# Adaptive layer norm block on one core: preparation joined with the projections, modulation applied by ScalarE, values stored without ones

## The chip, the cores and the metric

One core of a Trainium2 chip runs the whole program in one launch. The metric is the device time in microseconds (us). TensorE (PE) multiplies matrices, VectorE (DVE) and ScalarE (ACT) work on tiles, GpSimd (POOL) works on tiles in on-chip memory, and SyncE (SP) issues transfers (DMAs). All tensors are float32; some operands of matmuls are marked fp32r.

## The reference, cut to what matters

A batch of 8 sequences of 1024 tokens with 256 channels goes through a 16-head attention and a two-layer windowed block, each behind a modulated layer norm. The change concerns the first part:

```python
x = L0_attn_x                                            # 8 x 1024 x 256
mod = (_silu(L0_c) @ L0_wmod).reshape(8, 6, 1, -1)
sa, ca, ga, sb, cb, gb = (mod[:, 0], ..., mod[:, 5])
ga = (2 * (ga >= 0) - 1) * jnp.maximum(jnp.abs(ga), 0.25)   # gb likewise
h = _layernorm(x, axis=-1) * (1 + ca) + sa
# attention of h:
q = x @ wq.T                      # 16 heads of 16 channels, rotated by an angle that depends on the head
k = x @ wk_a.T @ wk_b.T           # through 64 latent channels, rotated too
v = x @ wv_a.T @ wv_b.T
attn = softmax(q k^T / 4)
x = x + ga * ((attn @ v) @ wo.T)
```

The angle depends on the head, not on the token, so the rotation is folded into the weights.

## The kernel before

The program is a row of blocks. At the end of a block all engines meet, and the block's stores must have landed.

**setup** loads the weights, transposes them on TensorE, rotates `wq` and `wkb` on VectorE, computes the 8 x 1536 modulation and stores it in DRAM (`mod_d`), and prepares a table `trl` for the later windowed block. Every engine waits for all 23 loads (`loaded`, `total`).

**projections** goes over 16 chunks of 512 tokens. For each chunk n, SP loads `pj_x` (512 KB) and `pj_mod` (a broadcast of two rows of `mod_d`). VectorE makes the statistics in 12 dependent steps (L365 to L88) and normalizes into `pj_xn` (L498). GpSimd multiplies by 1 + ca and adds sa in two passes (L534) into `pj_hm`. TensorE transposes it (L554, eight 128x128 turns), ScalarE copies `pj_hT` out (L601), TensorE makes the 128 latent channels (L563), q (L570), k (L577) and v (L585). ScalarE copies the high parts of q and k (L611, L613) and v (L619). VectorE subtracts to get the low parts (L504, once for q and once for k). SP stores four tiles of parts (L468, 512 KB each) and v (L471). Every value head of 16 channels is stored with 16 ones beside it, so that one matmul later gives both the weighted sum and the softmax's denominator; `pj_v` is therefore 1024 KB a chunk. VectorE works two chunks ahead with the normalization, in slices between the two low parts, and TensorE turns one chunk ahead.

**full_attention** goes over 32 groups (batch x 4 heads) of 16 steps. TensorE computes the scores twice, once for the row maxima (L803, reduced by VectorE at L923) and once transposed (L822) for ScalarE's exponential (L896), and then the sums with the values (L837). SP loads q, k and v of group n + 2 while group n runs. GpSimd has only the split of the next stage's weights there (L1205, L1210), once, in group 9.

**attention_out** (16 chunks of 512 tokens) and four later blocks follow; the change leaves their code as it is.

The lines around which the change turns:

```python
def body(n, p, following=True):                       # TensorE, projections
    pe.wait_ge(h_ready.sem, h_ready.upto(n))
    ...                                               # latents L563, q L570
    pe.wait_ge(lat_ready.sem, lat_ready.upto(n))
    ...                                               # k L577
    if following:
        turn(n + 1, 1 - p)
    ...                                               # v L585
```

Of the kernel before, what the change touches and what calls it, by code (L numbers as in the profile page):

```python
# [7 lines left out]
ALU = mybir.AluOpType  # L8
# [7 lines left out]
P = 128  # L16
# [116 lines left out]
def build(nc, a, out):  # L133
    with ExitStack() as ctx:
# [5 lines left out]
        v_d = dram("v_d", [B, N, NH * 2 * HD])  # L140
# [52 lines left out]
def setup(nc, a, ident, w, mod_d, trig_d, hi_d):  # L193

    with ExitStack() as ctx:
        def sb(name, shape, dt=F32):
            return ctx.enter_context(nc.sbuf_tensor(name, shape, dt))

        def sem(name):
            return ctx.enter_context(nc.semaphore(name))  # L200

        wq_r = sb("wq_r", [P, KT, D])
        wo_r = sb("wo_r", [P, KT, D])
        wa_r = sb("wa_r", [P, D])
        wb_r = sb("wb_r", [P, KT, P])
        rope = sb("rope_b", [P, 2, P])
        ropeq = sb("rope_q", [P, 2, P])
        ta, tb = sb("rope_ta", [P, KT, P]), sb("rope_tb", [P, KT, P])
        cs = sb("c_rows", [B, D])
        ce = sb("c_exp", [B, D])  # L210
        cT = sb("c_T", [P, KT, B])
        wmod = sb("wmod_sb", [P, KT, 6 * D])
        mods = sb("mods", [B, 6, D])
        ga, gs = sb("guard_a", [B, 2, D]), sb("guard_s", [B, 2, D])
        trig = sb("trig_base", [P, NW, 4 * DH])
        qks = sb("qk_scales", [P, DEPTH, 4 * DH])
        trl = sb("trig_scaled", [P, DEPTH, NW, 4 * DH])
        zrow = sb("zero_rows", [B, P])
        ps = [ctx.enter_context(nc.psum_tensor(f"ps_set{i}", [P, 512], F32)) for i in range(8)]
        loaded, turned, steps, silu, stored = (sem("set_loaded"), sem("set_turned"), sem("set_steps"),  # L220
                                               sem("set_silu"), sem("set_stored"))
        small, modm = sem("set_small"), sem("set_mod")
        n_loads = [0]

        with nc.Block() as block:
            @block.sync
            def _(sp):
                def load(dst, src):
# [25 lines left out]
                for h in hi_d:  # L254
                    sp.dma_start(h[:, 0, :], zrow[:]).then_inc(stored, 16)
# [1907 lines left out]
```

## Time and profile before

| what | value |
|---|---|
| time, median of 3 runs | 4484.74 us (4481.17 to 4498.85) |
| time of the profiled execution | 4477.03 us |
| its span, first to last instruction | 4475.2 us |
| mean granted TensorE clock, as a share of full | 0.973 |
| busy: PE / DVE / ACT / POOL | 92% / 80% / 62% / 36% |
| HBM read and written | 178.56 MB and 111.21 MB |

The span is 1.8 us shorter than the time of the same execution. Busy shares are means over all blocks, and the blocks have different limits, so the stretch of the projections has to be looked at alone. A granted clock of 1.00 is 2.4 GHz and 0.50 is 1.2 GHz.

### The profile page before, as it was taken

To read this page: it belongs to the slowest core of one execution; us is meant where nothing else is said; L and a number is where in the kernel's file an instruction comes from. 1 tells how busy PE (TensorE), PEld (TensorE's weight loads), DVE (VectorE), ACT (ScalarE), POOL (GpSimd) and SP (SyncE) were. 2 spreads that over 40 slices of the span, in tenths; PEclk is the share of its full clock that TensorE was granted. 3 is DMA by queue.
4 is the path that set the end of the run, shared out by engine and by line. 5 is a ranking of instruction groups with operands and counts; after the bars stand their busy time and mean duration, and the time that the engine had idled before them with its cause. 6 is when DMAs were issued, how large, how long until landed. Compare 5 with 4: busy or idle time off the path is not lost. (4 is left out here: it accounts for less than half of the span.)

```text
span 4475.2 us, 79984 instructions
## 1 busy us (share of the span) xinstructions
PE 4134.2 (92%) x26906; PEld 2636.3 (59%) x26906; DVE 3575.0 (80%) x7980; ACT 2776.3 (62%) x6215; POOL 1622.9 (36%) x2440
## 2 busy tenths in 40 slices
PE   4959999999999996499999998999899999998998
PEld 2523333333333334377777776888777777777887
DVE  5669999999999976788888886556588888895665
ACT  1428888888888882067766665444567666664443
POOL 2400001000000002456655554454456555554555
PEclk8969999999999998799999999999999999999999
DMA  5952434434343315610000010212010000101321
GB/s 186 375 113 45 65 52 87 59 49 64 49 61 57 52 26 183 190 42 25 25 28 25 26 39 16 89 48 67 19 45 25 28 25 27 40 16 58 88 72 56
DMA packets 368445, 295.91 MB, mean 66 GB/s; under 512 B 66393, under 2 KB 325289, under 8 KB 368049
## 3 DMA queue, kind: packets, MB, share of 16 engines
q1 hardware_dynamic: 368048, 290.93, 26.5%
q8 instruction: 212, 3.47, 0.3%
q14 instruction: 185, 1.51, 0.1%
HBM read 178.56 MB, written 111.21 MB: 65 GB/s over the span
## 5 line engine op out<-in xcount | busy, mean ns | idle before, releaser
L896 ACT ACTIVATE fa_P<-fa_pS 128x512 f32<-128x512 f32 x2048 | 1111.7, 595 | 316.9 <-PE fa_pS L822 267.3
L923 DVE TENSOR_REDUCE fa_mx<-fa_pR 128x2 f32<-128x1024 f32 x1024 | 1205.7, 1221 | 92.8 <-PE fa_pR L803 78.2
L1683 POOL TENSOR_TENSOR wa_pn<-wa_pr,wa_ri 128x512 f32<-128x512 f32 (+1 forms) x512 | 673.2, 1316 | 493.8 <-DVE wa_ri L1735 493.6
L1621 ACT ACTIVATE wa_pr<-wa_sm,wa_mn 128x256 f32<-128x256 f32 (+1 forms) x1024 | 496.7, 488 | 177.7 <-DVE wa_mn L1726 151.4
L837 PE MATMUL fa_pO<-fa_P,fa_V 128*32 128x512 f32 x4096 | 546.5, 606 | 0.2 <-ACT fa_P L896 0.2
L822 PE MATMUL fa_pS<-fa_Q,fa_K 50*128 50x512 f32 x2048 | 508.1, 493 | 41.3 <-ACT fa_P L896 11.0
L822 PEld LDWEIGHTS fa_pS<-fa_Q,fa_K 50*128 50x128 f32 x2048 | 191.4, 184 | 517.2 <-ACT fa_P L896 431.4
L803 PE MATMUL fa_pR<-fa_K,fa_Q 48*128 48x512 f32 x2048 | 430.7, 464 | 57.2 <-DMA fa_K<-parts_d 38.3
L1150 POOL TENSOR_TENSOR ao_xn<-ao_xn,ao_mod 128x1024 f32<-128x1024 f32 x16 | 37.6, 2348 | 1092.1 <-DVE ao_xn L1115 1092.1
L1472 PE MATMUL wa_pQK<-wa_wqkv,wa_xT 128*128 128x512 f32 x1536 | 422.9, 412 | 6.3 <-DVE wa_qa L1772 6.3
L1726 DVE CUSTOM_DVE_ANT_0 wa_sm<-wa_pS,wa_mask 128x256 f32<-128x256 f32 (+1 forms) x1024 | 356.9, 402 | 19.0 <-issue 14.4
L1631 ACT COPY wa_pT<-wa_pP 128x512 f32<-128x512 f32 (+1 forms) x512 | 284.9, 557 | 126.7 <-PE wa_pP L1519 126.5
L2021 POOL TENSOR_TENSOR ff_u<-ff_uF,ff_u 128x512 fp32r<-128x512 f32 x192 | 247.6, 1290 | 287.0 <-ACT ff_u L2124 283.2
L803 PEld LDWEIGHTS fa_pR<-fa_K,fa_Q 48*128 48x128 f32 x2048 | 196.6, 189 | 246.7 <-DVE fa_mx L923 152.1
L2116 ACT ACTIVATE ff_gl<-ff_pG,ff_b 128x512 f32<-128x512 f32 x192 | 131.9, 687 | 334.1 <-PE ff_pG L2067 333.8
L1519 PE MATMUL wa_pP<-ident,wa_pn 128*128 128x128 f32 x1920 | 307.9, 281 | 18.5 <-ACT wa_pT L1631 15.3
L2067 PE MATMUL ff_pG<-ff_hT,ff_w 128*128 128x512 f32 x1152 | 302.9, 398 | 8.4 <-DVE ff_hT L1972 8.4
L1472 PEld LDWEIGHTS wa_pQK<-wa_wqkv,wa_xT 128*128 128x128 f32 x1536 | 273.2, 191 | 54.6 <-DVE wa_qa L1772 7.7
L1506 PE MATMUL wa_pS<-wa_kT,wa_qT 64*128 64x256 f32 (+1 forms) x2048 | 277.1, 388 | 7.4 <-DVE wa_mn L1726 2.2
L1531 PE MATMUL wa_pO<-wa_pT,wa_V 128*64 128x128 f32 x3840 | 268.0, 281 | 4.3 <-ACT wa_pT L1631 4.3
L1519 PEld LDWEIGHTS wa_pP<-ident,wa_pn 128*128 128x128 f32 x1920 | 209.3, 141 | 100.4 <-issue 82.5
L2082 PE MATMUL ff_pY<-ff_w,ff_u 128*128 128x256 f32 x2176 | 266.2, 283 | 0.0
(185 smaller groups left out, 7104.5 us busy)
## 6 DMA issues: line engine op xcount, KB each, us to landing
parts_d<-pj_parts SPq DMA_DIRECT2D x64, 512.0 KB, 5.5
fa_Q<-parts_d SPq DMA_DIRECT2D x192, 128.0 KB, 4.3
fa_K<-parts_d SPq DMA_DIRECT2D x192, 128.0 KB, 7.5
v_d<-pj_v SPq DMA_DIRECT2D x16, 1024.0 KB, 8.5
fa_V<-v_d SPq DMA_DIRECT2D x32, 512.0 KB, 9.9
pj_x<-in_L_attn_x SPq DMA_DIRECT2D x16, 512.0 KB, 7.7
fa_Q<-fa_nrow SPq DMA_DIRECT2D x512, 2.0 KB
att_d<-fa_att SPq DMA_DIRECT2D x64, 128.0 KB, 2.5
```

The source lines that it names most:

```text
L803: last = nc.tensor.matmul(slot[:, e, :], Qs[at:at + SROWS, s, a, q * P:(q + 1) * P], Ks[at:at + SROWS, s, a, kh * HALF:(kh + 1) * HALF], s ...
L822: nc.tensor.matmul(pS[:, (s * exped.per + u + e) % T, :], Ks[at:at + SROWS + 2, s, a, kb * P:(kb + 1) * P], Qs[at:at + SROWS + 2, s, a, ha ...
L837: last = nc.tensor.matmul(pO[h * 32:(h + 1) * 32, :], V[:, s, kb, h, :], Pr[:, k % 2, h, :], start=(kb == 0), stop=(kb == KB - 1))
L896: nc.scalar.activation(Pr[:, k % 2, h, :], pS[:, (s * exped.per + u) % T, :], ACT.Exp).then_inc(exped.sem, 1)
L923: nc.vector.tensor_reduce(mx[:, q // QB, :, a, q % QB, kh], row_slot(), AX.X, ALU.max).then_inc(row_free, 1)
L1472: last = nc.tensor.matmul(out, xT[:, x, k, :], wqkv[:, y, k, j * INNER:(j + 1) * INNER], start=(i == 0), stop=(i == len(products) - 1))
L1519: last = nc.tensor.transpose(pP[:, at:at + P], pn[:, hp % 2, hh, side * WIN:(side + 1) * WIN], ident[:])
L1621: last = nc.scalar.activation(pr[:, hp % 2, hh, lo:], sm[:, hp % 2, hh, lo:], ACT.Exp, bias=mn[:, p, h:h + 1], scale=-1.0, accum_out=rs[:, ...
L1631: nc.scalar.copy(pT[:, hp % 2, :, side:2].rearrange("p h w t -> p h (w t)"), pP[:].rearrange("p (h k) -> p h k", h=2)[:, :, side * P:2 * P ...
L1683: nc.gpsimd.tensor_tensor(pn[:, hp % 2, :, lo:], pr[:, hp % 2, :, lo:], inv, ALU.mult).then_inc(s["weighted"].sem, 1)
L1726: last = nc.vector.tensor_tensor_reduce(out=sm[:, hp % 2, hh, lo:], in0=pS[:, hh, (hp % 2) * 2 * WIN + lo:(hp % 2 + 1) * 2 * WIN], in1=mas ...
L2067: last = nc.tensor.matmul(ps[:, j % 2, :], w1[:, x, k, part, j * P:(j + 1) * P], hT[:, p, y, k, :], start=(i == 0), stop=(i == len(product ...
```

## The change

There is no separate preparation block. Its loads, turns and rotations are written into the projections' block, in front of and between the chunks. Eight of the loads are issued by ScalarE's queue. Shift and scale of the attention are computed as columns (channels on partitions, one column for each batch), so that ScalarE can apply them as bias and scale while it copies the turned chunk out, in two halves (L545 of the new kernel). GpSimd has nothing left to do in the projections, and `pj_mod` and `pj_hm` are gone. The other four modulation rows are made in chunk 1, the guard of the gates follows there, and the table `trl` is made in chunks 4 and 6. The matmuls of k use rows 0 to 63 of the array and those of v rows 64 to 127, and they are written alternately. The turn of chunk n + 1 stands right behind the latents. SP stores q's parts before k's are ready. Values are stored as they are (512 KB a chunk); in full_attention GpSimd writes the ones once, and spreads each group's values between them (`fa_Vc` to `fa_V`).

```diff
-            setup(nc, a, ident, w, mod_d, trig_d, hi_d)
-            projections(nc, a["L0_attn_x"], ident, w, mod_d, parts_d, v_d)
+            projections(nc, a, ident, w, mod_d, trig_d, hi_d, parts_d, v_d)
...
+                for n in range(NC):                              # SP
+                    store(n, n % 2)
+                    if n + R < NC:
+                        load(n + R)
+                    if n == PREPARED_AT:
...
+                        sp.dma_start(trig_d.rearrange("l w p c -> p (l w) c"),
+                                     trl[:].rearrange("p l w c -> p (l w) c")).then_inc(prepared, 16)
...
+                stats_of(0, 0, range(LN_INCS))                   # DVE
+                normalize(0, 0)
...
+                nc.vector.tensor_copy(w.shift[:], cols[:, 0]).then_inc(vector_made, 1)
+                nc.vector.tensor_scalar(w.scale[:], cols[:, 1], 1.0, None, ALU.add).then_inc(vector_made, 1)
...
+                stats_of(1, 1, range(LN_INCS))
+                normalize(1, 1)
...
                     last.then_inc(lat_done.sem, 1)              # PE
+                    if n + 1 < NC:
+                        turn(n + 1, 1 - p)
...
                     for m in range(KT):
+                        nc.tensor.matmul(pK[:, m, :], w.wkb[0:LAT, m * P:(m + 1) * P], lat[0:LAT, p, :],
+                                         start=True, stop=True).then_inc(k_done.sem, 1)
+                        for bank, t in (((0, 2), (0, 3)), ((1, 0), (1, 1)))[m]:
+                            last = nc.tensor.matmul(pL[:, bank, (t % 2) * D:(t % 2 + 1) * D],
+                                                    lat[LAT:P, p, t * P:(t + 1) * P], w.wvb[LAT:P, :],
+                                                    start=True, stop=True)
+                        last.then_inc(v_done.sem, 1)
...
-                    nc.scalar.copy(hT[:, p], pH[:]).then_inc(h_ready.sem, 1)
+                    for k in range(KT):
+                        nc.scalar.activation(hT[:, p, k, :], pH[:, k, :], ACT.Identity, bias=w.shift[:, k, b:b + 1],
+                                             scale=w.scale[:, k, b:b + 1]).then_inc(h_ready.sem, 1)
...
+                def spread(n, s):                                # GpSimd, full_attention
+                    pool.wait_ge(v_in.sems[s], v_in.upto(n))
+                    if n >= NB:
+                        pool.wait_ge(summed.sem, summed.upto(n - NB))
+                    nc.gpsimd.tensor_copy(V[:, s].rearrange("p k h c -> p (k h) c")[:, :, 0:HD],
+                                          Vc[:, s].rearrange("p k (h c) -> p (k h) c", c=HD)).then_inc(v_spread.sem, 1)
```

TensorE's order in a chunk of the projections, before (chunk 1):

```order
L563 MATMUL pj_pL<-pj_hT,waT 128x512 [waits pj_v_ready,pj_h_ready]
L563 MATMUL pj_pL<-pj_hT,waT 128x512
L570 MATMUL pj_pQ<-pj_hT,wqT 128x512 [waits pj_lows]
L570 MATMUL pj_pQ<-pj_hT,wqT 128x512 x3
L577 MATMUL pj_pK<-pj_lat,wkbT 128x512 [waits pj_lows,pj_lat_ready]
L577 MATMUL pj_pK<-pj_lat,wkbT 128x512
L554 MATMUL pj_pH<-ident,pj_hm 128x128 [waits pj_h_ready,pj_modded]
L554 MATMUL pj_pH<-ident,pj_hm 128x128 x7
L585 MATMUL pj_pL<-wvbT,pj_lat 128x256 [waits pj_v_ready]
L585 MATMUL pj_pL<-wvbT,pj_lat 128x256 x3
```

The same of the change, in its chunk 3:

```order
L473 MATMUL pj_pL<-pj_hT,waT 128x512 [waits pj_v_ready,pj_h_ready]
L473 MATMUL pj_pL<-pj_hT,waT 128x512
L449 MATMUL pj_pH<-ident,pj_xn 128x128 [waits pj_h_ready,pj_normed]
L449 MATMUL pj_pH<-ident,pj_xn 128x128 x7
L485 MATMUL pj_pQ<-pj_hT,wqT 128x512 [waits pj_lows]
L485 MATMUL pj_pQ<-pj_hT,wqT 128x512 x3
L494 MATMUL pj_pK<-pj_lat,wkbT 128x512 [waits pj_v_ready,pj_lows,pj_lat_ready]
L497 MATMUL pj_pL<-wvbT,pj_lat 128x256 x2
L494 MATMUL pj_pK<-pj_lat,wkbT 128x512
L497 MATMUL pj_pL<-wvbT,pj_lat 128x256 x2
```

The turn (L554, now L449) has moved from behind k to behind the latents, it waits for VectorE's `pj_normed` where it waited for GpSimd's `pj_modded`, and v's matmuls stand between those of k.

VectorE's order at the start of the change, from the column form of the modulation to the second chunk's statistics:

```order
L383 TENSOR_TENSOR wkbT<-rope_ta,rope_tb 64x128 [waits pj_steps]
L416 COPY mod_shift<-pj_pQ 128x16 [waits pj_tensor_made]
L417 TENSOR_SCALAR mod_scale<-pj_pQ 128x16
L378 TENSOR_TENSOR rope_ta<-pj_pK,rope_q 128x256 [waits pj_vector_made,pj_tensor_made]
L379 TENSOR_TENSOR rope_tb<-pj_pK,rope_q 128x256 [waits pj_steps]
L380 TENSOR_TENSOR wqT<-rope_ta,rope_tb 128x256 [waits pj_steps]
L381 TENSOR_TENSOR rope_ta<-pj_pK,rope_q 128x256 [waits pj_steps]
L382 TENSOR_TENSOR rope_tb<-pj_pK,rope_q 128x256 [waits pj_steps]
L383 TENSOR_TENSOR wqT<-rope_ta,rope_tb 128x256 [waits pj_steps]
L194 BN_STATS pj_stats<-pj_x 128x6 [waits pj_loaded1]
```

The statistics of chunk 1, on which TensorE's turn of chunk 1 waits, stand behind the rotation of `wq`; before, they stood behind the normalization of chunk 0 alone, in a block of their own.

## Rows read from the trace of the kernel before

**Rows 1.** Busy time by stretch: PE, PEld, DVE, ACT, POOL, then clock, DMA share, GB/s.

```profile
core 0: us, PE busy (x) PEld busy (x) DVE busy (x) ACT busy (x) POOL busy (x), PEclk, DMA share, GB/s
100.00:200.00 100.00, 94.28 (x302) 49.38 (x300) 69.68 (x248) 44.31 (x57) 46.73 (x20) 1.00 1.04 377
270.00:308.00 38.00, 25.32 (x67) 9.44 (x67) 35.69 (x34) 0.00 (x0) 0.00 (x0) 0.50 0.44 67
613.30:656.60 43.30, 42.01 (x268) 14.44 (x266) 40.29 (x42) 35.79 (x66) 0.00 (x0) 1.00 0.37 56
699.90:743.20 43.30, 42.05 (x268) 14.44 (x266) 40.33 (x43) 35.82 (x67) 13.90 (x12) 1.00 0.34 56
1750.00:1800.00 50.00, 30.95 (x114) 24.09 (x115) 46.62 (x123) 5.06 (x5) 21.82 (x11) 0.81 0.79 242
```

**Rows 2.** Timeline from 25 to 80 us: start, duration, engine, line, operation.

```profile
25.19 4.49 DVE L310 TENSOR_TENSOR trig_scaled<-trig_base,qk_scales 128x2048 f32<-128x2048 f32 x2 [23.41 <-DMA qk_scales<-in_L_ffn_k_scale]
...
54.82 1.40 DVE L365 BATCH_NORM_STATS2 pj_stats<-pj_x 128x6 f32<-128x256 f32 x4 [3.82 <-DMA pj_mod<-mod_d]
...
58.86 1.38 DVE L498 TENSOR_SCALAR pj_xn<-pj_x,pj_mv,pj_rstd 128x256 f32<-128x256 f32 x4
...
62.93 2.18 DVE L85 SCALAR_TENSOR_TENSOR pj_tmp<-pj_rstd 128x4 f32<-128x4 f32 x1
...
65.14 1.97 PE L554 MATMUL pj_pH<-ident,pj_hm 128*128 128x128 f32 x8 [24.82 <-POOL pj_hm L534]
...
68.27 3.53 PE L563 MATMUL pj_pL<-pj_hT,waT 128*128 128x512 f32 x4 [1.16 <-ACT pj_hT L601]
...
79.57 3.14 SPq L468 DMA_DIRECT2D parts_d<-pj_parts  x4
```

**Rows 3.** Timeline of one chunk of the projections, 150 to 162 us.

```profile
150.51 1.23 DVE L504 TENSOR_TENSOR pj_parts<-pj_pK,pj_parts 128x1024 fp32r<-128x1024 f32 x1
...
152.24 1.38 DVE L498 TENSOR_SCALAR pj_xn<-pj_x,pj_mv,pj_rstd 128x256 f32<-128x256 f32 x4
152.58 3.60 PE L570 MATMUL pj_pQ<-pj_hT,wqT 128*128 128x512 f32 x8
...
156.01 1.88 PE L577 MATMUL pj_pK<-pj_lat,wkbT 128*128 128x512 f32 x4
...
156.12 2.35 POOL L534 TENSOR_TENSOR pj_hm<-pj_xn,pj_mod 128x1024 f32<-128x1024 f32 x1
...
157.93 1.01 ACT L613 CAST pj_parts<-pj_pK 128x1024 fp32r<-128x1024 f32 x1 [0.65 <-PE pj_pK L577]
...
158.53 1.09 PE L554 MATMUL pj_pH<-ident,pj_hm 128*128 128x128 f32 x8 [0.64 <-POOL pj_hm L534]
...
159.46 1.89 PE L585 MATMUL pj_pL<-wvbT,pj_lat 128*128 128x256 f32 x8
...
160.87 1.23 DVE L504 TENSOR_TENSOR pj_parts<-pj_pK,pj_parts 128x1024 fp32r<-128x1024 f32 x1
```

**Rows 4.** Groups by line, 100 to 250 us: VectorE's wait for the loads.

```profile
L365 DVE BATCH_NORM_STATS2 pj_stats<-pj_x 128x6 f32<-128x256 f32 x44 | 15.5, 414 | 28.9 <-DMA pj_mod<-mod_d 28.9
```

**Rows 5.** DMA issues, 100 to 200 us: count, KB each, median us to landing.

```profile
v_d<-pj_v SPq DMA_DIRECT2D x10, 1024.0 KB, 8.6
pj_x<-in_L_attn_x SPq DMA_DIRECT2D x10, 512.0 KB, 7.7
```

**Rows 6.** Timeline of TensorE in full_attention, 422 us.

```profile
422.07 0.46 PE L822 MATMUL fa_pS<-fa_Q,fa_K 50*128 50x512 f32 x2
422.46 1.07 PE L837 MATMUL fa_pO<-fa_P,fa_V 128*32 128x512 f32 x8
```

**Rows 7.** Timeline of the projections' end, 231 to 246 us.

```profile
231.88 1.22 DVE L504 TENSOR_TENSOR pj_parts<-pj_pK,pj_parts 128x1024 fp32r<-128x1024 f32 x1
...
236.28 1.25 SPq L471 DMA_DIRECT2D v_d<-pj_v  x1
...
243.86 1.76 DVE L911 MEMSET fa_K<- 32x2048 f32 x1 [10.76 <-PEq L451]
```

**Rows 8.** Line 2108, ScalarE with bias and scale: min, median, max ns.

```profile
L2108 ACT ACTIVATE ff_hT<-ff_pH,ff_lb,ff_lg x64: 767/776/788, 2774.3 to 4438.8; 128x512 fp32r<-128x512 f32 x64
```

More of the change, by code:

```diff
@@ L435, in rounds @@
-        def rounds(eng, body):
-            for n in range(R):
-                body(n, n)
-            with eng.Fori(1, NC // R - 1) as i:
-                for r in range(R):
-                    body(i * R + r, r)
-            for n in range(NC - R, NC):
-                body(n, n % R, following=n + 2 < NC)
-        def later(n):
-            return not isinstance(n, int) or n >= 2
-        def again(n):
-            return not isinstance(n, int) or n >= 1
+        TRIG_AT, ROWS_AT, GUARD_AT, PREPARED_AT = (4, 6), 1, 3, 8
@@ L470, in store @@
                     sp.wait_ge(v_ready.sem, v_ready.upto(n))
[L471 to L480 removed]
+                    sp.dma_start(rows(v_d, n), vs[:, p]).then_inc(stored.sems[p], 16)
@@ L580, in body @@
-                    if following:
-                        turn(n + 1, 1 - p)
-                    if again(n):
-                        pe.wait_ge(v_ready.sem, v_ready.upto(n - 1))
-                    for bank, t in ((0, 2), (0, 3), (1, 0), (1, 1)):
-                        last = nc.tensor.matmul(pL[:, bank, (t % 2) * D:(t % 2 + 1) * D],
-                                                lat[:, p, t * P:(t + 1) * P], w["wvb"][:], start=True, stop=True)
-                        if t % 2 == 1:
-                            last.then_inc(v_done.sem, 1)
@@ new lines, in _ @@
+                pe.wait_ge(cols_in, 16)
+                pe.wait_ge(vector_made, SILU)
+                for i in range(2 * KT):
+                    for k in range(KT):
+                        last = nc.tensor.matmul(pMod[:, i * B:(i + 1) * B], wmod[:, k, i * P:(i + 1) * P],
+                                                cT[:, k, :], start=(k == 0), stop=(k == KT - 1))
+                last.then_inc(tensor_made, 1)
+                for k in range(KT):
+                    for m in range(KT):
+                        last = nc.tensor.transpose(pQ[:, 0, k * D + m * P:k * D + (m + 1) * P],
+                                                   wo_r[:, m, k * P:(k + 1) * P], ident[:])
@@ L593, in _ @@
+                last.then_inc(tensor_made, 1)
+                for n in range(NC):
+                    body(n, n % 2)
             @block.scalar
             def _(act):
-                act.wait_ge(ones.sem, 1)
                 def h_out(n, p):
                     act.wait_ge(turned.sem, turned.upto(n))
-                    if later(n):
+                    if n == 0:
+                        act.wait_ge(vector_made, COLS_OUT)
+                    if n >= 2:
                         act.wait_ge(q_done.sem, q_done.upto(n - 2))
-                    nc.scalar.copy(hT[:, p], pH[:]).then_inc(h_ready.sem, 1)
@@ new lines, in body @@
+                    if n == ROWS_AT:
+                        for bank in range(2):
+                            act.wait_ge(tensor_made, ROWS_DONE + bank)
+                            nc.scalar.copy(mods[:, 2 * bank:2 * bank + 2, :],
+                                           pL[0:B, bank, :].rearrange("p (r c) -> p r c", r=2)).then_inc(scalar_made, 1)
+                act.dma_start(cs[:], a["L0_c"]).then_inc(c_in, 16)
+                act.dma_start(wa_r[0:LAT, :], a["L0_attn_wk_a"]).then_inc(weights_in, 16)
@@ L623, in _ @@
+                nc.scalar.copy(w.wvb[LAT:P, :], pB[LAT:P]).then_inc(scalar_made, 1)
                 h_out(0, 0)
-                pairs(act, body)
+                act.wait_ge(tensor_made, WO_TURNED)
+                nc.scalar.copy(w.wo[:].rearrange("p k n -> p (k n)"), pQ[:, 0, :]).then_inc(scalar_made, 1)
+                for n in range(NC):
+                    body(n, n % 2)
 def full_attention(nc, a, ident, parts_d, v_d, att_d, trig_d, wh):
```

474 lines of the change are left out of this document (218 added, 256 removed).

## The prediction

> **What bounds the kernel now.** I read the busy time by stretch first. The change works in the first 270 us of 4475; from there on only the values' loads and a copy on GpSimd differ. The projections' stretch has TensorE at 94.28 of 100 us, and at the same time the DMA share at 1.04 with 377 GB/s [rows 1]. Two resources are full, so a mean doesn't say which one sets the pace, and the timeline has to.
>
> In the timeline of the start the reader should see how much of it is waiting. VectorE begins its real work at 25.19, when the last of the small loads is there; its first statistics begin at 54.82, the first turn at 65.14, the latents of chunk 0 at 68.27, and chunk 0's parts are ready for storing at 79.5 [rows 2]. No chunk is made in these 80 us but one.
>
> In the timeline of a chunk the last low part comes at 150.51 and again at 160.87 [rows 3]: 10.36 us a chunk. From the first (chunk 0, 79.5) to the last (chunk 15, 231.88 + 1.22 = 233.1 [rows 7]) it is 153.6 us for 15 chunks, 10.24 each. In a chunk TensorE waits only for GpSimd's `pj_hm` (0.64 us), and VectorE waits 28.9 us in all for loads [rows 4], the sign of the full DMA queue. The last low part ends at 151.74, is followed by two small steps and the normalization (to 153.62), and GpSimd ends only at 158.47, 4.85 us later [rows 3].
>
> **The start, step by step.** The preparation runs beside the first loads. The first DMA of the program is issued in the first microsecond (both queues start empty). x of chunk 0 is the second on SP's queue; a 512 KB load takes 7.7 us when the queues are full [rows 5], so it is there by about 8.9, and sooner on an empty queue. The sigmoid's short chain stands before it on VectorE, behind eight DMA issues on ScalarE; I take 8.5 for the first statistics, with 7 and 11 as ends. Statistics and normalization take 60.24 - 54.82 = 5.42 us [rows 2]: 13.9. The turn takes 1.97 at the low clock [rows 2]: 15.9. Then come 16 small matmuls for the shift and scale columns. No row shows them; their weights are 128 columns, as in a turn, which costs 1.97 / 8 = 0.25 us each at most, so I take 0.21 each, 3.4 us (ends 1.6 and 4): 19.4. VectorE makes the columns (0.4), rotates `wq` (six operations on 256 columns; the 1024-column one takes 1.23 [rows 3], so between 0.31 and 1.23 each, I take 0.45): 22.5. Statistics and normalization of chunk 1 come behind it, 5.42: 27.9. TensorE's q of chunk 0 stands behind the turn of chunk 1, so all of this is on the path. Turn 1.97: 29.9. q has eight records, 0.87 apart at the low clock (four took 3.53 [rows 2]) and 0.43 at the full one (eight took 3.60 [rows 3]); with three low and five high 4.8: 34.7. k 1.9, copy 1.0, low part 1.2, and the gaps between engines 0.2: **39.0 instead of 79.5, a gain of 40.5 us.**
>
> **The period of a chunk.** Where GpSimd's 4.85 us disappear, a shorter loop closes, because the turn now stands in front of q: low part of k (n) to normalization (n + 2) to turn (n + 2) to q (n + 1) to low parts (n + 1). Its terms, all [rows 3]: two steps and normalization 1.88, handover 0.05, turn 0.93 (158.53 to 159.46), q 3.43 (152.58 to 156.01), its drain and handover 0.2, ScalarE's copy 1.01, handover 0.03, low part of q 1.23, four small steps 0.8 (13 of them fill 56.22 to 58.86 [rows 2], 0.2 each), low part of k 1.23. Sum 10.8. The branch through k comes to 0.3 us less if k and v run beside each other: k 1.88 in place of low part and steps. I take **10.75, 0.5 us more a chunk than now**, although TensorE's own work falls to 0.93 + 3.43 + 1.72 + 1.9 = 8.0 us and a chunk's transfers fall from 3840 to 3072 KB (8.3 us at 377 GB/s). Both cease to bound. ScalarE's copy with bias and scale costs 0.776 for 512 columns [rows 8], 1.55 for both halves against 1.01; it lies under q's 3.43 and costs nothing. If q were not there, it would cost 0.54.
>
> TensorE's next latents wait until ScalarE has emptied v's bank, behind k's copy: 0.6 us after the k copy. They take 1.7, in all 2.3, and the normalization comes 3.1 after that copy (1.23 + 1.88), so this wait is hidden with 0.8 to spare.
>
> Chunks 14 and 15 have no normalization behind them: 10.4 and 8.7. Thus 13 x 10.75 + 19.1 = 158.9 against 153.6, **a loss of 5.3**.
>
> **Single insertions.** In chunk 1 eight records of the modulation rows (3.6, as q) and a small copy delay the next latents by about 4.8, of which 0.8 is the slack above: **loss 4**. The gates' seven small operations fit under chunk 2's latents, turn and q (7 x 0.45 = 3.2 of 6). The table's operation takes 4.49 / 2 = 2.25 us [rows 2] and fits into VectorE's wait before low part of q (2.9 us: from the normalization 0.05 + 0.93 + 3.43 + 0.2 + 1.01 = 5.6, less 2.7 of statistics). The table's store of 2048 KB at chunk 8 is 5.4 us of full transfer; the queue has 0.9 MB of room a chunk, so x of chunk 13 comes late: **loss 2** (ends 0 and 5).
>
> **The end.** Now the last v store is issued 3.2 us after the last low part, behind four parts, and the next block starts 10.76 after it [rows 7]. After, only k's two stores stand in front (1.6), and v has half the bytes: a 512 KB transfer lands in 7.7 under load, 1024 KB in 8.6 [rows 5]. About 8 in all: **gain 2.8**.
>
> **full_attention.** GpSimd spreads 512 elements a partition in each of 32 groups. Its 12 operations in group 9 took 13.90 us, 1.16 on average, and the stretch beside them was the same as one without: VectorE 40.33 against 40.29, TensorE 42.05 against 42.01 [rows 1]. That work covers the spread, and since the copy of group n + 2 can be made a whole group ahead, nobody waits: **0** (uncovered, 32 x 1.16 = 37). In the projections it was otherwise: a 128x4 operation of VectorE took 2.18 us beside GpSimd's [rows 2], where its likes take 0.2; this goes away and is in the 0.2 used above. The GPSIMD Engine Reference of the Trainium skill (section Key points) says that GpSimd shares its memory interfaces with VectorE, and that VectorE suffers in two-port modes or with two inputs from that memory. The trace agrees in both places, since a maximum over the matmuls' output is neither. By that rule the ones that GpSimd writes at the block's start may delay VectorE's memsets (L911), which no row shows; I leave it at 0, with an end of 2.
>
> **Sum.** 40.5 - 5.3 - 4 - 2 + 2.8 = 32.0. The profiled execution took 4477.0, the median of the runs is 7.7 higher; 4484.7 - 32.0 = **4452.7, 0.7% faster**. A measurement of this kernel can tell about 0.5%, 22 us.
>
> **A point against the change.** The array now changes twice a chunk between full rows and half rows. In full_attention such a change stands between L822 and L837, 0.39 us from start to start [rows 6]; so a switch costs at most 0.39. The one behind v lies in TensorE's wait. The one before k eats the 0.3 us by which k's branch is shorter. The sum stays. TensorEngine Tiling of the Trainium skill (Key Properties) says that changing the mode drains the engine. By that rule the k branch becomes 0.1 longer than the other, and the sum 1 to 2 us worse.
>
> **Rivals.**
> 1. *k and v don't run beside each other.* For it: the records of a float32 matmul come in pairs, and v has shorter ones than k, so a strict order could hold them apart. Against: L837 with eight records of 0.43 ends in 1.07 and L822 with two in 0.46 [rows 6], so tiles do overlap. v's first two then stand before k's second half, k's branch grows by 0.86 less 0.3, 15 x 0.55 = 8: **4461**.
> 2. *The loop is shorter than I make it*, because the turn finds the normalization ready or the loads don't wait: bounded by TensorE's work and ScalarE's copies, 9.7 a chunk, 15 x 1.0 = 15 less: **4438**.
> 3. *TensorE's clock falls (slower).* Its busy share in the projections falls from 94% to 8.0 / 10.75, 75%. The next stages show 62% (30.95 of 50) with a clock of 0.81, and 67% with 0.50 [rows 1]. At 1.2 GHz turn, q and k double: 0.93 + 3.43 + 1.72 = 6.1 us a chunk. It decides from 32 / 6.1, 5.2 chunks. With a clock of 0.81, six chunks, the result is 4489, no difference; with all at 1.2 GHz **4548**, slower. Against: the waits are 1 to 2 us each.
> 4. *The spread isn't covered:* 37 us, **4490**, no difference.
>
> **Chances.** My sum 0.50 (its own range 4442 to 4465), rival 1 0.17, rival 2 0.13, rival 3 0.12 (0.05 of it without a measurable difference), rival 4 0.05, other losses 0.03. Faster by over 0.5% is below 4462.3: 0.46 + 0.10 + 0.13 = 0.69. Slower: 0.07 + 0.03 = 0.10. Same: 0.21. The range takes in rivals 1 and 2 and half of the unmeasurable ones: 4430 to 4482.
>
> **What would show it.** Right: chunk 0's last low part at 36 to 42 us; 10.5 to 11 us from one k low part to the next; TensorE waiting at the turn for `pj_xn` about 0.8 us a chunk; VectorE without waits for `pj_x` except near chunk 13; DMA share about 0.8; first L923 about 30 us earlier; group period 43.3 as before. Wrong: a first store much after 42, a period over 11.3, a granted clock of 0.50 within the projections, or a group period over 43.5.

## The result, and the profile after

The changed kernel takes 4461.25 us, the median of 8 runs (4450.39 to 4469.25), against 4487.39 of the kernel before beside it (8 runs, 4477.29 to 4498.85). The ratio is 0.9936, with a 95% interval of 0.9919 to 0.9954: 0.64% faster. The forecast was 4452.7, in a range of 4430 to 4482. The profiled execution took 4465.89 us, with a span of 4464.1 and a mean granted clock of 0.969 (0.973 before). It reads 165.98 MB and writes 102.81 MB, 21.0 MB less in all.

Two profiled executions differ by 11.1 us only, the medians by 26. So I lay the two traces beside each other stretch by stretch:

| stretch | before | after | difference | forecast |
|---|---|---|---|---|
| start to chunk 0's last low part | 79.33 | 43.11 | -36.2 | -40.5 |
| 15 intervals between k's low parts | 153.8 | 164.6 | +10.8 | +11.3 |
| last low part to `fa_K`'s memset | 10.75 | 7.60 | -3.2 | -2.8 |
| memset to the first exponential | 64.6 | 64.0 | -0.6 | 0 |
| groups 0 to 30 of full_attention | 1343.6 | 1343.0 | -0.6 | 0 |
| group 31, the last | 42.88 | 55.90 | +13.0 | 0 |
| attention_out and the later blocks | 2780.3 | 2786.0 | +5.6 | 0 |

The first three rows sum to -28.6 us, where I had forecast -32. The rest should not have moved, and two of its rows did. I take the start first. The timeline of the changed kernel, 17 to 43 us:

```profile
17.46 0.29 DVE L410 TENSOR_SCALAR rope_q<-rope_b 128x256 f32<-128x256 f32 x1 [4.44 <-DMA wo_r<-in_L_attn_wo]
17.49 0.69 PE L510 MATMUL pj_pL<-ident,wa_r 128*128 128x128 f32 x2 [14.50 <-DMA wo_r<-in_L_attn_wo]
...
19.25 1.91 PE L449 MATMUL pj_pH<-ident,pj_xn 128*128 128x128 f32 x8
20.96 3.42 PE L524 MATMUL pj_pQ<-c_T,wmod_sb 128*128 128x8 f32 x16
...
32.67 1.22 PE L449 MATMUL pj_pH<-ident,pj_xn 128*128 128x128 f32 x8 [2.62 <-DVE pj_xn L364]
33.68 5.21 PE L485 MATMUL pj_pQ<-pj_hT,wqT 128*128 128x512 f32 x8
...
41.89 1.22 DVE L370 TENSOR_TENSOR pj_parts<-pj_pK,pj_parts 128x1024 fp32r<-128x1024 f32 x1
```

The bracket to look at is the one behind L510: TensorE waits 14.50 us, until the last of the seven weights, `wo_r`, has landed. Chunk 0 has been normalized since 13.02, and is turned only at 19.25. The DMA issues of 0 to 20 us show why (queue, count, KB, median us to landing):

```profile
wq_r<-in_L_attn_wq ACTq DMA_DIRECT2D x1, 256.0 KB, 10.5
wo_r<-in_L_attn_wo ACTq DMA_DIRECT2D x1, 256.0 KB, 12.5
rope_b<-in_rope ACTq DMA_DIRECT2D x1, 128.0 KB, 9.6
```

In the kernel before, the order in which the loads landed didn't matter, because every engine waited for all of them (VectorE until 25.19 [rows 2]). A steady chunk in the timeline:

```profile
151.66 0.69 PE L494 MATMUL pj_pK<-pj_lat,wkbT 64*128 64x512 f32 x1
151.66 0.70 PE L497 MATMUL pj_pL<-wvbT,pj_lat 64*128 64x256 f32 x2
...
152.86 1.22 DVE L370 TENSOR_TENSOR pj_parts<-pj_pQ,pj_parts 128x1024 fp32r<-128x1024 f32 x1 [3.19 <-ACT pj_parts L559]
...
153.05 0.59 PE L494 MATMUL pj_pK<-pj_lat,wkbT 64*128 64x512 f32 x1
...
153.68 1.01 ACT L561 CAST pj_parts<-pj_pK 128x1024 fp32r<-128x1024 f32 x1 [0.84 <-PE pj_pK L494]
...
154.58 0.16 DVE L88 SCALAR_TENSOR_TENSOR pj_rstd<-pj_tmp,pj_rstd 128x4 f32<-128x4 f32 x1
154.72 1.23 DVE L370 TENSOR_TENSOR pj_parts<-pj_pK,pj_parts 128x1024 fp32r<-128x1024 f32 x1
155.32 1.95 PE L473 MATMUL pj_pL<-pj_hT,waT 128*128 128x512 f32 x4 [1.67 <-ACT pj_v L565]
...
156.44 1.38 DVE L364 TENSOR_SCALAR pj_xn<-pj_x,pj_mv,pj_rstd 128x256 f32<-128x256 f32 x4
...
157.88 1.10 PE L449 MATMUL pj_pH<-ident,pj_xn 128*128 128x128 f32 x8 [0.61 <-DVE pj_xn L364]
158.81 3.60 PE L485 MATMUL pj_pQ<-pj_hT,wqT 128*128 128x512 f32 x8
```

This answers [rows 3]. Where the chunk before had TensorE waiting for GpSimd, it now waits for ScalarE's copy of v's first bank, which stands behind k's (1.67), and for the normalization (0.61). L494 and L497 start in the same instant: the two row tiles do run side by side. The low part of k starts at 154.72, 0.03 after ScalarE's copy of k has ended (154.69), and VectorE's small steps (L88) end there too, so both branches of the loop close together, as forecast. The period is 10.68. The end of the projections:

```profile
215.26 1.76 DVE L896 MEMSET fa_K<- 32x2048 f32 x1 [7.60 <-PEq L288]
```
 For [rows 4], the wait of 28.9 us for loads is gone from VectorE, and it waits for q's copy instead (groups by line, 100 to 200 us):

```profile
L370 DVE TENSOR_TENSOR pj_parts<-pj_pQ,pj_parts 128x1024 fp32r<-128x1024 f32 x10 | 12.2, 1224 | 28.7 <-ACT pj_parts L559 28.7
L194 DVE BATCH_NORM_STATS2 pj_stats<-pj_x 128x6 f32<-128x256 f32 x32 | 11.2, 410 | 1.2 <-DMA pj_x<-in_L_attn_x 1.2
```

Busy time by stretch, with the columns of [rows 1]:

```profile
100.00:200.00 100.00, 77.67 (x294) 40.52 (x294) 65.53 (x224) 47.28 (x66) 0.00 (x0) 1.00 0.87 303
584.00:627.30 43.30, 42.06 (x268) 14.40 (x266) 40.35 (x43) 35.87 (x67) 0.62 (x1) 1.00 0.34 51
1634.00:1678.00 44.00, 36.33 (x146) 8.90 (x146) 0.68 (x2) 25.96 (x49) 0.00 (x0) 0.58 0.01 3
```

The second row is a group with GpSimd's spread in it (0.62 us), and it is as long as any. The third row is the last group. Its clock is 0.58 on average. In the trace before, the same work had a clock of 1.00:

```profile
1652.00:1695.00 43.00, 31.82 (x203) 9.24 (x202) 2.17 (x8) 35.70 (x66) 0.00 (x0) 1.00 0.03 7
```

So 13 us of what the change gains are missing in this one execution. Nothing that the change edits stands there.

### The profile page after: what moved, and what is told of

It is laid out like the page before. It is cut to its first block and busy times, and to the rows that moved or that the text cites. A ratio compares the mean times of both kernels' runs of the same rounds, so it can differ in the third digit from the quotient of the medians.

```text
span 4464.1 us, 79549 instructions
## 1 busy us (share of the span) xinstructions
PE 4130.9 (93%) x26918; PEld 2629.4 (59%) x26918; DVE 3555.6 (80%) x7972; ACT 2784.3 (62%) x6236; POOL 1568.3 (35%) x2441
## 3 DMA queue, kind: packets, MB, share of 16 engines
HBM read 165.98 MB, written 102.81 MB: 60 GB/s over the span
## 5 line engine op out<-in xcount | busy, mean ns | idle before, releaser
L822 PE MATMUL fa_pO<-fa_P,fa_V 128*32 128x512 f32 x4096 | 555.6, 615 | 0.0
L805 PE MATMUL fa_pS<-fa_Q,fa_K 50*128 50x512 f32 x2048 | 512.0, 497 | 41.9 <-ACT fa_P L881 11.2
L805 PEld LDWEIGHTS fa_pS<-fa_Q,fa_K 50*128 50x128 f32 x2048 | 192.6, 185 | 526.5 <-ACT fa_P L881 439.7
L786 PE MATMUL fa_pR<-fa_K,fa_Q 48*128 48x512 f32 x2048 | 429.5, 463 | 55.2 <-DMA fa_K<-parts_d 36.2
L753 POOL COPY fa_V<-fa_Vc 128x512 f32<-128x512 f32 x32 | 19.6, 613 | 1243.8 <-DMA fa_Vc<-v_d 1243.8
L786 PEld LDWEIGHTS fa_pR<-fa_K,fa_Q 48*128 48x128 f32 x2048 | 195.8, 188 | 244.4 <-DVE fa_mx L908 151.8
```

The source lines that it names most:

```text
L786: last = nc.tensor.matmul(slot[:, e, :], Qs[at:at + SROWS, s, a, q * P:(q + 1) * P], Ks[at:at + SROWS, s, a, kh * HALF:(kh + 1) * HALF], s ...
L805: nc.tensor.matmul(pS[:, (s * exped.per + u + e) % T, :], Ks[at:at + SROWS + 2, s, a, kb * P:(kb + 1) * P], Qs[at:at + SROWS + 2, s, a, ha ...
L822: last = nc.tensor.matmul(pO[h * 32:(h + 1) * 32, :], V[:, s, kb, h, :], Pr[:, k % 2, h, :], start=(kb == 0), stop=(kb == KB - 1))
```

## Experiments

Ten kernels ran, on three chips. Each is compared with the kernel before on its own chip: 4494.21 us there for the first four (17 runs, 4483.32 to 4507.37), 4485.94 for the next four (17 runs, 4476.25 to 4498.6), 4495.03 for the last two (9 runs, 4477.92 to 4510.06).

**1. k and v one behind the other.** The changed kernel, its k and v again over all 128 rows, with the other half of the weights zero.

```diff
-  w.wkb[0:LAT, m * P:(m + 1) * P], lat[0:LAT, p, :],
+  w.wkb[:, m * P:(m + 1) * P], lat[:, p, :],
-  lat[LAT:P, p, t * P:(t + 1) * P], w.wvb[LAT:P, :],
+  lat[:, p, t * P:(t + 1) * P], w.wvb[:],
```

> The changed kernel with k's and v's matmuls over all 128 rows of the array (weights filled up with zeros), so that they run one behind the other in the same order. Theory of the chunk's loop (low part of k, normalization, turn, q, then the slower of two branches): k's second half now stands behind v's first two products, k's branch grows from 0.3 us shorter than VectorE's to about 0.6 longer, and the period of a chunk goes from 10.68 to 11.2 us, some 8 us more in all. Rival, that VectorE's own work or the transfers set the 10.68: the period stays within 0.1 us. Rival, that TensorE's work sets it: the period grows by the whole 1.7 us to 12.4.

One execution took 4469.18 us. The period is 11.35 (13 of 15 intervals). The timeline of TensorE:

```profile
151.99 3.60 PE L487 MATMUL pj_pQ<-pj_hT,wqT 128*128 128x512 f32 x8
155.42 1.02 PE L496 MATMUL pj_pK<-pj_lat,wkbT 128*128 128x512 f32 x2
156.28 1.03 PE L499 MATMUL pj_pL<-wvbT,pj_lat 128*128 128x256 f32 x4
157.14 1.02 PE L496 MATMUL pj_pK<-pj_lat,wkbT 128*128 128x512 f32 x2
158.00 1.03 PE L499 MATMUL pj_pL<-wvbT,pj_lat 128*128 128x256 f32 x4
```

k now takes 2.74 us from its first start to its end (155.42 to 158.16), against 1.98 in the changed kernel (151.66 to 153.64), 0.76 more. But it also starts 0.10 earlier behind q: from q's first start to k's it is 3.43 here, without a change between full and half rows, and 3.53 with it (158.81 to 151.66 + 10.68). So k's branch is 0.66 longer, and the period grows by 0.67: k's branch had no slack, and the loop through the low parts sets the period. Rival 1 is what the kernel would be without the row tiles. A switch costs 0.10 us, where I had 0.39 as the end. The fifteen intervals are 8.0 us longer together, as expected, though only because the modulation rows cost 1.7 less here (experiment 10).

**2. The turn behind q.** The changed kernel, with the turn of chunk n + 1 behind q of chunk n, and ScalarE's copy of it behind q's.

```diff
                     last.then_inc(lat_done.sem, 1)
-                    if n + 1 < NC:
-                        turn(n + 1, 1 - p)
...
                     last.then_inc(q_done.sem, 1)
+                    if n + 1 < NC:
+                        turn(n + 1, 1 - p)
```

> The changed kernel with the turn of chunk n + 1 behind q of chunk n instead of in front of it, and ScalarE's copy of the turned chunk behind the copy of q. Theory of the loop: the chain from the normalization to the low parts no longer passes through q, and what is left is TensorE's own row: latents 1.7, q 3.4, turn 0.9, k and v 1.7, and the wait of 1.9 for v's bank to be emptied, 9.7 us a chunk instead of 10.68. Chunk 0 is ready 3 us earlier, since q of chunk 0 no longer waits for the normalization of chunk 1. Together 15 to 18 us less. Rival, that VectorE or the transfers set the pace: the period stays at 10.6 or more and only the 3 us at the start come.

4440.27 us (4 runs, 4432.18 to 4454.84), a ratio of 0.9885 (0.9857 to 0.9913) to the kernel before. The period is 9.85, chunk 0 is ready at 40.11, and `fa_K`'s memset stands at 201.12 instead of 215.26. That is 14.1 us, just under the 15 to 18 expected. TensorE waits no more for `pj_xn`. What it waits for is one line (groups, 90 to 190 us):

```profile
L473 PE MATMUL pj_pL<-pj_hT,waT 128*128 128x512 f32 x40 | 19.5, 611 | 16.6 <-ACT pj_v L565 16.6
```

TensorE's work and this wait fill the chunk. So the place of the turn, one of the parts of the change, is what made a chunk slower.

**3. The values alone.** The kernel before, with values stored as they are and spread by GpSimd in full_attention; preparation, modulation and order stay as they were.

```diff
-            v_d = dram("v_d", [B, N, NH * 2 * HD])
+            v_d = dram("v_d", [B, N, D])
...
+                        spread(n, s)                             # GpSimd, full_attention
```

> The kernel before with one part of the change alone: values stored without ones, and spread by GpSimd in full_attention. Theory: of the change's gain this brings little; a chunk's transfers fall from 3840 to 3328 KB, VectorE's wait for loads (28.9 us over 14 chunks) shrinks, and the loop of two chunks through GpSimd stays, so the period goes from 10.36 to 10.0 to 10.3, 0 to 5 us in all, and the group period in full_attention stays at 43.27. Rival, that the transfers set the pace before: the period falls with the bytes to 9.3 or less, 15 us. Rival, that the spread hurts: group period over 43.5.

4486.98 us (10 runs, 4474.3 to 4495.16), a ratio of 0.9981 (0.9967 to 0.9995): 2 to 15 us faster. The trace says 7.4: `fa_K`'s memset at 236.49 instead of 243.86, intervals of 9.91 on average instead of 10.25. That is more than the 0 to 5 us that I had expected. A group of full_attention takes 43.31 on average (43.28 before), so the spread is free here too. What replaced the wait for loads is seen in VectorE's groups, 100 to 200 us, first in the kernel before and then here:

```profile
L85 DVE SCALAR_TENSOR_TENSOR pj_tmp<-pj_rstd 128x4 f32<-128x4 f32 x27 | 4.3, 159 | 0.6
...
L85 DVE SCALAR_TENSOR_TENSOR pj_tmp<-pj_rstd 128x4 f32<-128x4 f32 x30 | 25.3, 842 | 0.7
...
L365 DVE BATCH_NORM_STATS2 pj_stats<-pj_x 128x6 f32<-128x256 f32 x40 | 14.0, 413 | 0.4 <-DMA pj_mod<-mod_d 0.4
```

and by two rows of its timeline:

```profile
152.69 2.36 POOL L532 TENSOR_TENSOR pj_hm<-pj_xn,pj_mod 128x1024 f32<-128x1024 f32 x1
...
152.87 2.19 DVE L85 SCALAR_TENSOR_TENSOR pj_tmp<-pj_rstd 128x4 f32<-128x4 f32 x1
```

A step that takes 0.16 us elsewhere takes 2.19, and ends with GpSimd's pass. VectorE is "busy" for 95.39 of 100 us in this kernel (69.68 before), with less than a chunk more of work in the stretch; L85, at 0.84 on average against 0.159, makes up 21 of the 26 us. This doesn't set the pace here, as TensorE is at 98.26 of 100. The GPSIMD Engine Reference of the Trainium skill (Key points) names two inputs from the shared memory as one of two cases in which the two engines contend, and L85 reads the same tile twice; the trace agrees.

**4. The last group kept busy.** The changed kernel, with four more products a step from step 3 on in the last group of full_attention, into a bank that nobody reads then.

```diff
+                def keep_busy(s, k):
+                    for e in (0, 1, 0, 1):
+                        at = e * TOP
+                        nc.tensor.matmul(pR[:, e, 1, :], Ks[at:at + SROWS, s, 0, 0:P],
+                                         Ks[at:at + SROWS, s, 0, 0:HALF], start=True, stop=True)
...
+                        if is_last(n) and k >= 3:
+                            keep_busy(s, k)
                         scores(n, s, k, 1)
```

> The changed kernel with four extra products of keys with keys in each of the last group's steps 3 to 15, written where nobody reads; they are no part of the computation. In the profiled execution of the changed kernel the granted clock fell to 0.50 at 1634 us, within the last group, which has no row scores, and the group took 55.9 us; before it stayed at 1.00 and the group took 42.9. Theory: the last group's thinner stream of matmuls leaves it to chance whether the clock falls, this chance is about 13 us of the scatter of both kernels, and with the extra products it does not fall: last group 43 us in the profile, the times of all rounds within about 6 us, and a median some 5 us below the changed kernel's. Rival, that the fall has another cause: the last group takes 55 us in some executions and the scatter stays at 19 us.

4452.79 us (6 runs, 4450.9 to 4457.24), a ratio of 0.9911 (0.9894 to 0.9929). The last group takes 42.83, its clock is 1.00 (busy time by stretch):

```profile
1625.00:1668.00 43.00, 38.02 (x253) 13.15 (x251) 2.34 (x8) 35.65 (x66) 0.00 (x0) 1.00 0.03 7
```

The scatter is 6.3 us, against 18.9 for the changed kernel. More work for TensorE, and not more time.

**5. The changed kernel again,** beside the next three.

> The changed kernel as it is, beside the next three on one chip. If the clock in the last group of full_attention falls in some executions and not in others, its times lie over at least 12 us, with a median 4 to 14 above that of the version whose last group is kept busy (4452.8). If the extra products of that version did nothing, the two have the same median and the same scatter.

4455.53 us (6 runs, 4450.4 to 4465.08), a ratio of 0.9931 (0.9914 to 0.9948). The scatter is 14.7 us; the lowest of its times and of the version with the busy group are 0.5 us apart (4450.4, 4450.9), the highest 7.8. Its profiled execution has yet another last group, 45.94 us with a clock of 0.89:

```profile
1624.00:1667.00 43.00, 32.68 (x186) 9.12 (x186) 1.53 (x5) 32.88 (x61) 0.00 (x0) 0.89 0.03 7
```

The medians of the two versions, 2.7 us apart, are from different chips, and the intervals of their ratios overlap; the median's gain of 4 to 14 that I had expected isn't shown.

**6. The weights first.** The changed kernel, SyncE's queue held after the first chunk of x and the first columns of `wmod`.

```diff
                 sp.dma_start(wmod[:, :, 0:2 * D], wmod_rows[:, :, 0:2 * D]).then_inc(cols_in, 16)
+                sp.wait_ge(weights_in, 16 * 7)
                 load(1)
```

> The changed kernel, SyncE's queue holding back all but the first chunk of x and the first columns of wmod until the seven weights have landed. If the weights' landing at 17.5 us sets the start, chunk 0's last low part ends at 37 to 38 us instead of 43.1, the period stays 10.68, and the time is 5 to 6 less than the changed kernel's on the same chip. If the first chunk's own statistics and turn or the modulation's columns set it, less than 2 us. If chunk 1's later load then sets it (rival), chunk 0's low part stays over 41.

Its DMA issues of 0 to 20 us, and its timeline:

```profile
wq_r<-in_L_attn_wq ACTq DMA_DIRECT2D x1, 256.0 KB, 4.3
wo_r<-in_L_attn_wo ACTq DMA_DIRECT2D x1, 256.0 KB, 4.7
```

```profile
12.92 1.97 PE L450 MATMUL pj_pH<-ident,pj_xn 128*128 128x128 f32 x8 [1.35 <-DVE pj_xn L365]
14.68 3.42 PE L525 MATMUL pj_pQ<-c_T,wmod_sb 128*128 128x8 f32 x16
```

`wo_r` lands 4.7 us after its issue instead of 12.5, the turn starts at 12.92 instead of 19.25, chunk 0 is ready at 37.58 instead of 43.1, and `fa_K`'s memset stands at 209.77, 5.1 us before that of run 5. So the two queues' sharing cost the start 5.1 (run 5's chunk 0 is ready at 42.68) to 5.5 us, more than the 4.1 by which my sum was off. The Trainium skill says in DMA: Bandwidth & Descriptors (Queues, rings and completion order) that each DMA engine goes round the queues that have work, a packet from each at a time. The trace of the changed kernel agrees. The packets of SyncE's queue (q1) and of ScalarE's (q10) from 8 to 14 us, with count, MB and share:

```profile
q1 hardware_dynamic: 794, 1.54, 67.8%
q10 hardware_dynamic: 796, 0.52, 34.2%
```

The packets are as many, but those of the weights are a third as large, so the weights get a quarter of the bytes. The time doesn't show the gain: 4459.27 us (6 runs, 4447.48 to 4468.68), with a scatter of 21 us. Its profiled execution has a last group of 53.6 us and two more falls of the clock in later blocks (below).

**7. The turn behind q, and v's first bank before k.**

```diff
-                    act.wait_ge(k_done.sem, k_done.upto(n))
-                    nc.scalar.copy(parts[:, p, 1, 0], pK[:]).then_inc(hi_ready.sem, 1)
                     for bank in range(2):
                         j = 1 - bank
+                        if bank == 1:
+                            act.wait_ge(k_done.sem, k_done.upto(n))
+                            nc.scalar.copy(parts[:, p, 1, 0], pK[:]).then_inc(hi_ready.sem, 1)
```

> The changed kernel with the turn behind q, and ScalarE emptying v's first bank ahead of k's copy. With the turn behind q alone the period was 9.85, and TensorE waited 1.66 of it at L473 for that bank behind k's copy. If that wait closes the loop, the period falls by 1.3 to 1.5, to the transfers' own floor: 3072 KB at 377 GB/s, 8.3 to 8.7 us; the time is then 15 to 22 below 4440. If the transfers at 337 GB/s (share 0.96) are the bound already (rival), it stays over 9.5.

4434.34 us (4 runs, 4423.86 to 4439.73), a ratio of 0.9872 (0.9851 to 0.9893). That is 5.9 below run 2, not the expected 15 to 22, and the intervals of the two ratios overlap; the gain is seen in the trace alone, where the memset stands 18.0 earlier, but the last group took 55.16 us (44.44 in run 2's). Seven of the fifteen intervals are 8.3 to 8.5, chunk 0 is ready at 36.08, and `fa_K`'s memset stands at 183.1, 31.7 before that of run 5. Now the transfers are full, at a share of 1.04 (busy time by stretch), and a load closes the longest interval (one row of VectorE's timeline):

```profile
90.00:140.00 50.00, 44.64 (x180) 25.27 (x179) 39.19 (x144) 28.07 (x41) 0.00 (x0) 1.00 1.04 367
```

```profile
137.21 1.41 DVE L194 BATCH_NORM_STATS2 pj_stats<-pj_x 128x6 f32<-128x256 f32 x4 [6.84 <-DMA pj_x<-in_L_attn_x]
```

This is x of chunk 13. SyncE issues the table's store of 2048 KB at 119.1, needs 3.48 us for the next issue and 5.50 for the four behind it, and comes to this load at 129.87; it lands at 137.2. The interval is 14.28. The store that cost nothing in the changed kernel, whose queue had room, stands here in front of a loss of some 6.

**8. The kernel before, its last group kept busy,** by the same edit as in 4.

> The kernel before, with four extra products a step from step 3 on in the last group of full_attention, written into a bank that nobody reads. If the fall of the clock in that group is a matter of chance that both kernels have, its scatter falls from 24 us (17 runs) to under 14, and its median lies 3 to 12 under that of the kernel before on the same chip. If only the changed kernel meets it (rival), the median stays within 2 us.

4484.11 us (12 runs, 4477.17 to 4488.35), a ratio of 0.9991 (0.998 to 1.0002). The scatter is 11.2 us against 22.4 of the kernel before beside it. The median is only 1.8 lower, less than I had expected. The trace of run 3, which is the kernel before but for the values, has a last group of 53.58 us with nothing added. So that kernel meets this fall too; the half as large scatter agrees for the kernel before itself, but its median execution doesn't lose by it.

**9. All together:** the edits of 4, 6 and 7 in one.

> The changed kernel with the turn behind q, v's first bank emptied ahead of k's copy, the other loads held back until the weights have landed, and the extra products in the last group of full_attention. If the parts add up: fa_K's first memset at 177 to 179 us (183.1 without the held loads, 214.8 in the changed kernel), the last group at 42.8, and a time 5 to 12 below that of the version without the last two (4434.3), 4422 to 4430. If the transfers of the projections are the bound (rival), what the earlier start gains is lost again in a queue that is full anyway: memset at 181 to 183, time over 4428.

4417.9 us (5 runs, 4416.93 to 4421.68), a ratio of 0.9829 (0.9802 to 0.9856). Chunk 0 is ready at 32.49, the memset stands at 180.06, the last group takes 42.91. The memset gains 3.0 us of the 3.6 by which chunk 0 is earlier than in 7, between what the two theories gave. The time is 4 us below the expected 4422 to 4430: beside the trace of run 7, the last group is 12.3 us shorter, and the clock falls at one of two later block ends instead of at both (5.7). The scatter is 4.8 us. It is the fastest of all versions, 1.7% under the kernel before.

**10. The modulation rows in chunk 5** instead of 1, and the guard in chunk 7.

```diff
-        TRIG_AT, ROWS_AT, GUARD_AT, PREPARED_AT = (4, 6), 1, 3, 8
+        TRIG_AT, ROWS_AT, GUARD_AT, PREPARED_AT = (4, 6), 5, 7, 8
```

> The changed kernel with the modulation rows made behind chunk 5 instead of chunk 1, and the gates' guard behind chunk 7. If their cost in chunk 1 (5.7 us over the period) is eight records of 0.43 us with their copy, and 1.7 more because the clock fell to 0.50 at that moment, then the interval from chunk 1 to 2 is 10.7, that from 5 to 6 is 14.5 to 15, and the clock stays at full at both places. If the insertion itself makes the clock fall wherever it is (rival), the interval from 5 to 6 is 16.2 to 16.5 with a stretch of 0.50 at about 97 us. The time of one execution says nothing of 1.7 us.

One execution took 4447.38 us. The interval from chunk 1 to 2 is 10.68, that from 5 to 6 is 16.39, to the hundredth what it was in chunk 1. My theory fell and the rival holds. The insertion, in TensorE's timeline:

```profile
93.94 5.29 PE L459 MATMUL pj_pL<-wmod_sb,c_T 128*8 128x512 f32 x8 [2.15 <-ACT pj_v L565]
```

Eight records (the trace shows a float32 matmul as two) take 5.29 us here, as they did in chunk 1, and the granted clock goes to 0.50 at 95 us. Ahead of them TensorE waits 2.15 us for ScalarE's copy. In version 9, where it waits 1.66 for it, the clock stays up and the same eight take 3.59:

```profile
40.27 3.59 PE L460 MATMUL pj_pL<-wmod_sb,c_T 128*8 128x512 f32 x8 [1.66 <-ACT pj_v L567]
```

The nine kernels that have these rows fall in two kinds: with a wait of 2.15 (the changed kernel and runs 2, 4, 5, 6 and 10) the eight took 5.22 to 5.29, and with one of 1.66 or 1.31 (runs 7, 9 and 1) 3.59. So the place isn't what matters, nor the insertion alone. How long TensorE stood before it goes with the fall in all nine, but the work ahead of it differs too (full rows in run 1, another order in 7 and 9), so that the wait is the cause isn't shown. Run 1 prices the insertion at full clock:

```profile
54.15 3.59 PE L461 MATMUL pj_pL<-wmod_sb,c_T 128*8 128x512 f32 x8 [1.31 <-ACT pj_v L567]
```

Its interval from chunk 1 to 2 is 15.37, 4.02 over its period of 11.35.

## Why the prediction was right, and where it was off

**The loop** was right, with no term of the period off by more than 0.2. The period was forecast at 10.75 and is 10.68; without what the insertion adds and 0.24 in one interval (below) the 15 intervals are 158.6 us (forecast 158.9). The experiments confirm its course: lengthening k's branch by 0.66 adds 0.67 (run 1), and taking the turn out of it brings 9.85 (run 2), near the 9.7 that rival 2 had as the bound. The row tiles run side by side, so rival 1 didn't come. The sentence that both TensorE and the transfers cease to bound holds too: 77.67 of 100 us and a share of 0.87.

**The start** was mis-sized by 4.1 us: 43.1 instead of 39.0. "x of chunk 0 is the second on SP's queue ... so it is there by about 8.9" was right (first statistics at 7.62, normalized at 13.02, forecast 13.9). The term that failed is "13.9. The turn takes 1.97", which lets the turn follow at once. On TensorE the turns of the weights stand ahead of it, and behind a wait for all seven; I had priced no landing on ScalarE's queue. The last came at 17.49, and the turn began at 19.25, 5.3 late; what follows it took 23.9 instead of 25.1, mainly because the turn of chunk 1 took 1.0 and not 1.97. Run 6 takes this away and gets 37.58, 1.4 under the forecast. The other terms of the start: modulation columns 3.42 (3.4), q 5.21 (4.8). That the joined preparation brings the 36 us is read from the two timelines; no run takes it alone, nor ScalarE's modulation.

**The insertions.** The modulation rows cost 5.71, not 4: the records were counted at full clock, and the clock fell in them; where it stayed up, the insertion cost 4.02 (run 1). The store of the table cost nothing, not 2, as a chunk with 303 GB/s left it room: it is issued at 141.22, and every interval that begins after it is 10.68, but for the last (8.98). The interval around it is 10.92, but its 0.24 come before the store, in a wait whose cause stays open:

```profile
135.08 1.38 DVE L364 TENSOR_SCALAR pj_xn<-pj_x,pj_mv,pj_rstd 128x256 f32<-128x256 f32 x4 [0.27 <-DVE pj_rstd L88]
```

That the misses of 1.7 and nearly 2 cancel in the sum is luck. The guard stands in chunk 3, not in chunk 1 as I wrote ahead of the result; the interval there is 10.75, so it costs 0.07.

**The end** gained 3.15 (2.8). **The spread** in full_attention cost nothing, as forecast: groups 1 to 30 take 43.28 before and after. Nor did the ones written at the block's start: VectorE's memsets beside them take 1.76, as behind them. Rival 4 didn't come.

**Sum of the parts:** 36.2 - 4.8 - 5.7 - 0.2 + 3.15 = 28.6, against 32.0. The ratio's interval is 20.6 to 36.3 us, which holds both.

**Rival 3, the clock,** was looked for in the wrong place. From chunk 1 of the projections on it stayed at 1.00 at 78% busy, but for 3.4 us at the insertion (54.0 to 57.4). In some executions and not in others it falls in three places that the change doesn't edit: the last group of full_attention, and two ends of blocks behind it. In the trace of the changed kernel these are +13.0 us and +5.1 us. The last group of the twelve profiled executions took 42.88, 42.89, 42.89, 44.44, 45.94, 53.58, 53.6, 55.16 and 55.90 us where nothing was added, and 42.83, 42.83 and 42.91 where TensorE was kept busy. TensorE has less to do there than in other groups, as no row maxima follow (TensorE's groups by line show L822, L805 and four of L830, and no L786). The groups before it have 42.06 of 43.3 us of TensorE's work, this one 31.82 of 43 even at full clock (before, 1652 to 1695). At two ends of blocks, near 2740 and near 4020 us, the traces show the same. Busy time of these stretches in run 6, and then in run 5:

```profile
2738.00:2762.00 24.00, 15.01 (x67) 11.68 (x64) 2.41 (x4) 6.51 (x9) 2.67 (x3) 0.50 0.13 39
4025.00:4049.00 24.00, 14.72 (x64) 11.45 (x59) 2.41 (x4) 6.52 (x9) 2.54 (x3) 0.50 0.33 93
```

```profile
2738.00:2762.00 24.00, 15.01 (x79) 11.84 (x78) 6.64 (x19) 8.03 (x12) 3.78 (x3) 0.83 0.13 39
4025.00:4049.00 24.00, 17.53 (x72) 13.93 (x71) 12.40 (x32) 9.74 (x14) 6.37 (x5) 0.86 0.33 94
```

From the windowed block's first matmul into `wa_pQK` to the end the executions with no stretch of over 11 us at 0.50 at these ends took 2581.5 to 2585.7 us, those with one 2587.6 to 2590.2, those with two 2594.6 to 2594.9. So 13 us and twice 5 are drawn anew in each execution, and make up most of a scatter of 15 to 25 us; groups 0 to 30 also vary, from 1342.6 to 1347.4. With more work in the last group it fell there in none of three traces (runs 4, 8 and 9), and without in six of nine; the scatter of the times shrank each time. What makes it fall in one execution and not in another stays open, and the two later places weren't tried.

## What to carry to other kernels

When two bounds of a loop fall at once, write out the shorter loop that closes next with each wait in it, and ask of every step that was moved whether it now stands inside: here one turn, ahead of q instead of behind it, cost 0.8 us a chunk, and together with the order of two copies 2.3 in the chunks that no load held up. When a preparation is joined with the main loop, every load in it gets a place on the path; hold back the bulk loads of the other queue until the small ones have landed. And before explaining a difference of 10 us between two traces, look whether the clock fell in a stretch that the change doesn't touch, and compare several executions.

## What the runs showed of the hardware

- Two queues took turns packet by packet (794 and 796 packets from 8 to 14 us), whatever the size of a packet (1.54 and 0.52 MB). 256 KB on the one with small packets took 12.5 us to land while the other held some 5 MB of loads, and 4.7 when the other was held back.
- A 128x4 operation of VectorE with two inputs from on-chip memory took 2.19 us beside a pass of GpSimd, and 0.16 otherwise. VectorE's busy share then reads 95%, where about the same work read 70%.
- A change between full rows and half rows of the array cost TensorE 0.10 us between q and k.
- In six kernels eight records behind a wait of 2.15 us ran at half clock for the most part (5.22 to 5.29 us); in three with a wait of 1.31 or 1.66 they took 3.59. The work ahead of the wait isn't the same in all, so this is a reading of one place and no rule.
- With four needless products a step the last group took 42.8 to 42.9 us in three traces; without them 42.9 to 55.9 in nine.
